# First hidden step by eight plain block products, token parts reordered at block ends, hidden sums widened and all put on VectorE

## The chip, the cores and the metric

The kernel runs on one core of one Trainium2 chip. The metric is the device time of one execution in microseconds (us); lower is better. Three runs of the kernel before gave 1954.87 to 1956.18 us, with a median of 1955.7 us. Engine names are those of the profile: PE is TensorE (PEld its weight load), DVE is VectorE, ACT is ScalarE, POOL is GpSimd, SP is SyncE, which issues the transfers.

## The reference

Each token vector goes through three feed-forward nets (two shared ones and one that its batch entry selects), the three results are weighted by a softmax gate and added to the token, and a linear layer of a chosen category is added on top.

```python
# x: (2, 2048, 512) read as 8 x 512 wide nets of hidden size F = 2048
s0 = relu(x @ swi[0]) @ swo[0]
s1 = relu(x @ swi[1]) @ swo[1]
eo = relu(x @ wi[type_label]) @ wo[type_label]
gate_in = concatenate([eo[:, 0], s0[:, 0], s1[:, 0]])
w = softmax(relu(gate_in @ g1) @ g2)
x = x + (eo * w[0] + s0 * w[1] + s1 * w[2])
out = x + (x @ W[cat_ids] + b[cat_ids])
```

All arrays are float32, and the kernel keeps float32 accuracy by splitting each factor of a product into a high part (rounded to the matmul's fp32r type) and a low part, the rest.

## The kernel before, in words

**Tiling.** The 4,096 tokens are worked in 4 blocks of 1,024. Each block runs through 12 steps: 3 nets by 4 slices of the hidden size, 48 steps `m` in all. A step multiplies tokens by a slice of the first weight matrix (the up products, PSUM banks `ups`), applies relu, and multiplies the hidden values by a slice of the second matrix (the down products, banks `rps`), which is summed into `ACC`.

**Products of blocks.** Every matrix product is done as a 2 by 2 product of blocks with seven block products instead of eight (Winograd's form). That needs sums of blocks on both sides: `XT` and `XS` of tokens, `PUS` and `PDS` of weights, and `HT` of hidden blocks. An up slice is done in two half steps `n = 2m` and `n = 2m + 1` of 512 tokens by 7 products of 6 matmuls each, and a down slice by 7 products of 12 matmuls. A step holds 168 matmuls of 128x512.

**Hidden blocks and their sums.** The seven up products of a half step are put together into four hidden blocks: `hid[:,0]` by a relu on ACT, `hid[:,2]` by `block_22` (L1227) on DVE and a relu, `HT[:,1]` by `block_21` (L1236) and a relu, `hid[:,1]` by a relu. From them `hidden_sum` (L737) makes four sums, `which` = 0 to 3, each of a half step's 128x512: those of half 0 on POOL, those of half 1 on DVE. Sum 1 reads sum 0, and sum 3 reads sum 1. `hidden_high` (ACT, L938) then rounds each of the seven inputs of the down products, 128x1024 for both halves, and `hidden_low` (DVE, L1186) takes the rest.

**Order within a step.** All engines run orders that are written out by hand. In step `m` PE goes through seven slots of two up products (of the half steps `a = 2m + 2` and `b = 2m + 3`, which belong to the next step) and one down product, by turns: `up(a,0)`, `up(a,1)`, `down(m-1,6)`; `up(a,2)`, `up(a,3)`, `down(m,0)`; `up(a,4)`, `up(a,5)`, `down(m,1)`; `up(a,6)`, `up(b,0)`, `down(m,2)`; and so on to `up(b,5)`, `up(b,6)` and `down(m,5)`. `up(a,6)` writes a bank that `block_22(a)` has to have read. `S(m)` below is the time at which `up(a,0)` starts.

On DVE a step is, in order: sums 0, 1 and 3, the preparation of weights where there is one (`up_low` L1166, `up_sums` L1322, `down_low` L1173), `hidden_low` 1, `second(0)` (the adding of `down(m-1,6)` into `ACC`, `add_sum`, L1205 and L1208), sum 2, `hidden_low` 2 and 6, `block_22(a)`, `hidden_low` 3, and so on. `first_product`, `seventh_product` and `chain` are ACT's copies of banks (L884, L890, L896), and L953 is its copy of the first down product of a step.

**Prepared weights.** In the first block, and again in steps 32 to 34 for a part of the weights, the high and low parts and block sums of weights are made on the chip and kept in HBM; later steps load them. POOL makes the sums of the down weights (`down_sums`, L779 to L788).

**Start.** Half step 0 needs no sums: it is done by the eight plain block products (`plain`, weights in `WD`), while the token and weight sums that half step 1 needs by seven products are made. The sums of its weights are made afterwards on POOL from `PF` (`first_up_sums`, L767), for the steps that load them later.

**Block ends.** In the last step of a block (`m` = 11, 23, 35; `start` in the code) the up products are already those of the next block, so its token parts (`token_high` L843, `token_low` L1157, tiles `XH`, `XL`) are made between the other work: `token_low` 3 ahead of the sums, 4 and 5 behind `second(0)`, 6 ahead of `block_22(a)`.

Of the kernel before, what the change touches and what calls it, by code (L numbers as in the profile page):

```python
# [12 lines left out]
P = 128  # L13
# [47 lines left out]

T_COUNT = [(1, 2, 3, 4), (1, 2, 4, 3)]
# [98 lines left out]
X_ORDER_FIRST = [0, 6, 3, 1, 2, 4, 5]  # L161
# [10 lines left out]
B12_USED = 3  # L172
# [27 lines left out]
def build(nc, xT, expert_id, category_id, wi, wo, swi, swo, g1, g2, W, bias, out):  # L200
# [13 lines left out]
    with ctx:  # L214
# [27 lines left out]
        PF = sb("PF", [P, 4, HB], F32, at=hh_at + 5 * 4 * KB)  # L242
# [25 lines left out]
        WS = sb("WS", [P, 4, 2, HB], F32R, at=r_at + 28 * KB)  # L268
        SR = sb("SR", [P, 4, HB], F32, at=r_at + 36 * KB)
# [39 lines left out]
        s_pf = sem("first_blocks_loaded")  # L309
# [26 lines left out]
        s_T = [sem("hidden_sums_0"), sem("hidden_sums_1")]  # L336
# [50 lines left out]
        def _(sp):  # L387
# [50 lines left out]
            def load_up(n, i):  # L438
# [3 lines left out]
                if weight_set(n // 2) == 0 and n % 2 == 0:  # L442
                    sp.wait_ge(s_wsk, 32)
# [114 lines left out]
            sp.dma_start(PF[:, :, :], swi[0, 0, :, :, :]).then_inc(s_pf, 16)  # L558
# [5 lines left out]
            blocks_up(1, None)  # L564
            blocks_up(2, None)
            blocks_down(0, None)
            sp.dma_start(g2s[:, :, :], g2_v).then_inc(s_g2, 16)
            keep_first(0)
            keep_first(1)
# [4 lines left out]
            keep_up(1, 0)  # L574
            keep_up(1, 1)
            blocks_up(3, experts)
# [3 lines left out]
            for m in range(STEPS):  # L580
# [4 lines left out]
                for i in range(PRODUCTS):  # L585
# [5 lines left out]
                    if m == 0 and i == 4:  # L591
                        keep_first_sums()
# [28 lines left out]
                    if True:  # L621
# [28 lines left out]
                        if m == 1 and i == 1:  # L650
                            load_ahead(1)
                        if m in (3, 4, 5) and i == 2:
                            keep_ahead(1, m - 3)
                        if m == 5 and i == 2:
# [65 lines left out]
        def hidden_sum(eng, N, half, which):  # L720

            before = PRODUCTS * (N - 1)
            h11, h12, h22 = (hid[:, q, half, :] for q in range(3))
            if N > 0:
                eng.wait_ge(s_dn, before + (3, 2, 4, 5)[which] + 1)
            if which == 0:
                eng.wait_ge(s_relu, 4 * (2 * N + half) + 4)
                dst, p, q, op = HT[:, 3, half, :], h22, h12, ALU.subtract
            elif which == 1:
                eng.wait_ge(s_T[half], 4 * N + T_COUNT[half][0])  # L730
                dst, p, q, op = HT[:, 2, half, :], HT[:, 3, half, :], h11, ALU.add
            elif which == 2:
                dst, p, q, op = HT[:, 4, half, :], h12, h11, ALU.subtract
            else:
                eng.wait_ge(s_T[half], 4 * N + T_COUNT[half][1])
                dst, p, q, op = HT[:, 5, half, :], HT[:, 1, half, :], HT[:, 2, half, :], ALU.subtract
            eng.tensor_tensor(dst, p, q, op).then_inc(s_T[half], 1)  # L737
# [15 lines left out]

        tail_banks = [aps[:, :], ups[2], ups[0], ups[1], rps[1][:, 0, :], rps[1][:, 1, :], rps[0][:, 0, :], rps[0][:, 1, :]]
# [6 lines left out]
        def _(pool):  # L761
            def first_up_sums():
# [979 lines left out]
```

## Time and profile before

| | |
|---|---|
| median of 3 runs | 1955.7 us (1954.87 to 1956.18) |
| the profiled execution | 1956.29 us |
| its span in the trace | 1954.4 us |
| PE busy | 1933.9 us, 99% |
| DVE busy | 1343.6 us, 69% |
| ACT busy | 981.7 us, 50% |
| POOL busy | 402.1 us, 21% |

The span is the time from the first to the last instruction that the trace shows, and the execution's own time is 1.9 us longer. Busy shares are means over the whole span: DVE is above 85% in the first quarter and near 60% after it. PEclk is the granted clock of PE as a share of its full speed.

### The profile page before, as it was taken

How to read it: one execution, taken by the hardware profiler on the slowest of the kernel's cores; microseconds unless marked ns; L12 is line 12 of the kernel's file. 1: busy time of each engine (PE TensorE's matmuls, PEld its weight loads, DVE VectorE, ACT ScalarE, POOL GpSimd, SP SyncE). 2: the span in 40 equal slices, each digit the busy share in tenths (PEclk: the TensorE clock that was granted, in tenths of full speed). 3: DMA queues.
4: the chain of work that ended last, by engine and by line, in shares of the span. 5: the costliest groups of instructions: out<-in, count | busy, mean ns of one | idle time of the engine just before them, and what ended most of it. 6: DMA issues, size and time to landing. Idle time of an engine off the chain costs nothing.

```text
span 1954.4 us, 25279 instructions
## 1 busy us (share of the span) xinstructions
PE 1933.9 (99%) x8510; PEld 1597.6 (82%) x8510; DVE 1343.6 (69%) x1508; ACT 981.7 (50%) x1438; POOL 402.1 (21%) x283
## 2 busy tenths in 40 slices
PE   7999999999999999999999999999999999999999
PEld 6888888887888888888888888888878888888887
DVE  8888888898576556565655545589975656555566
ACT  5766766756454334444554344456555433344342
POOL 3234224322211111331111111122321111111120
PEclk9999999999999999999999999999999999999999
DMA  6876777768876666786776676578777776656642
GB/s 219 300 292 249 292 279 295 278 242 304 277 256 217 204 204 215 266 293 211 261 258 204 193 224 209 189 278 295 267 279 257 239 228 221 216 182 211 224 156 97
DMA packets 192321, 468.29 MB, mean 240 GB/s; under 512 B 17476, under 2 KB 58436, under 8 KB 185924
## 3 DMA queue, kind: packets, MB, share of 16 engines
q1 hardware_dynamic: 192196, 466.69, 69.8%
q8 instruction: 70, 1.15, 0.2%
q14 instruction: 55, 0.45, 0.1%
HBM read 319.82 MB, written 146.80 MB: 239 GB/s over the span
## 4 chain that ended last, share of the span: by engine, by line
PE 73%; DVE 2%; DMA 1%; issue 1%; ACT 1%; SPq 0%; ACTq 0%; DVEq 0%
PE ups L1555 35%; PE rps L1555 35%; PE aps L1555 3%; DMA XT<-xT_kept 1%; DVE WD L1173 0%; DVE XL L1157 0%; DVE HL L1186 0%; DVE HT L737 0%; ACT XH L843 0%; ACT HH L938 0%; DVE ACC L1205 0%; DVE XT L1512 0%; ACT WD L874 0%; DVE XL L1518 0%; PE aps L1654 0%
## 5 line engine op out<-in xcount | busy, mean ns | idle before, releaser
L1555 PE MATMUL ups<-XH,WU 128*128 128x512 f32 x2660 | 878.0, 391 | 14.1 <-issue 4.4
L1555 PE MATMUL rps<-HH,WD 128*128 128x512 f32 x2672 | 876.5, 389 | 0.6 <-ACT rps L953 0.6
L1555 PEld LDWEIGHTS ups<-XH,WU 128*128 128x128 f32 x2660 | 501.7, 189 | 123.0 <-issue 11.0
L1555 PEld LDWEIGHTS rps<-HH,WD 128*128 128x128 f32 x2672 | 501.3, 188 | 105.4 <-DVE HL L1186 1.3
L1555 PE MATMUL rps<-HL,WD 128*128 128x512 f32 x1336 | 519.7, 389 | 0.0
L1555 PE MATMUL ups<-XL,WU 128*128 128x512 f32 x1330 | 519.3, 390 | 0.0
L737 POOL TENSOR_TENSOR HT<-hid 128x512 f32<-128x512 f32 x96 | 133.2, 1388 | 1316.8 <-PE rps L1555 1298.2
L1186 DVE TENSOR_TENSOR HL<-HT,HH 128x1024 fp32r<-128x1024 f32 x240 | 290.2, 1219 | 9.6 <-ACT HH L938 5.1
L1208 DVE SCALAR_TENSOR_TENSOR ACC<-rps,gw,ACC 128x1024 f32<-128x1024 f32 x126 | 161.6, 1282 | 196.6 <-PE rps L1555 196.3
L1555 PEld LDWEIGHTS rps<-HL,WD 128*128 128x128 f32 x1336 | 251.0, 188 | 52.1
L1555 PEld LDWEIGHTS ups<-XL,WU 128*128 128x128 f32 x1330 | 250.6, 188 | 51.5
L938 ACT ACTIVATE HH<-HT 128x1024 fp32r<-128x1024 f32 x240 | 252.4, 1053 | 26.8 <-DVE HT L737 25.2
L1205 DVE TENSOR_TENSOR ACC<-rps,ACC 128x1024 f32<-128x1024 f32 x124 | 151.4, 1221 | 103.0 <-PE rps L1555 102.9
L912 ACT ACTIVATE HT<-HT 128x512 f32<-128x512 f32 x95 | 60.1, 633 | 276.3 <-DVE HT L1236 276.3
L1227 DVE TENSOR_TENSOR hid<-ups,w 128x512 f32<-128x512 f32 x95 | 65.4, 688 | 123.4 <-PE ups L1555 123.4
L1186 DVE TENSOR_TENSOR HL<-hid,HH 128x1024 fp32r<-128x1024 f32 x96 | 131.3, 1368 | 20.0 <-ACT HH L938 20.0
L904 ACT ACTIVATE hid<-ups 128x512 f32<-128x512 f32 x95 | 56.4, 594 | 117.5 <-PE ups L1555 117.5
L896 ACT ACTIVATE u<-ups 128x512 f32<-128x512 f32 x95 | 56.8, 598 | 105.3 <-PE ups L1555 105.3
L890 ACT ACTIVATE w<-ups 128x512 f32<-128x512 f32 x95 | 55.9, 588 | 102.3 <-PE ups L1555 102.3
L938 ACT ACTIVATE HH<-hid 128x1024 fp32r<-128x1024 f32 x96 | 101.6, 1058 | 1.5
L884 ACT ACTIVATE ups<-ups 128x512 f32<-128x512 f32 x95 | 55.3, 583 | 81.5 <-PE ups L1555 78.3
L908 ACT ACTIVATE hid<-hid 128x512 f32<-128x512 f32 x95 | 60.1, 632 | 68.1 <-DVE hid L1227 68.0
(129 smaller groups left out, 1521.7 us busy)
## 6 DMA issues: line engine op xcount, KB each, us to landing
WU<-wu_kept SPq DMA_DIRECT2D x448, 256.0 KB, 3.5
WD<-wd_kept SPq DMA_DIRECT2D x224, 512.0 KB, 3.3
wd_kept<-WD SPq DMA_DIRECT2D x112, 512.0 KB, 3.5
wu_kept<-WU SPq DMA_DIRECT2D x31, 1024.0 KB, 4.9
wu_kept<-WU SPq DMA_DIRECT2D x31, 768.0 KB, 4.5
sums_kept<-ACC SPq DMA_DIRECT2D x28, 512.0 KB, 5.4
MB<-sums_kept SPq DMA_DIRECT2D x28, 512.0 KB, 5.7
XS<-in_x_dram SPq DMA_DIRECT2D x21, 512.0 KB, 5.8
```

Of the source, the lines that this page charges most:

```text
L737: eng.tensor_tensor(dst, p, q, op).then_inc(s_T[half], 1)
L890: act.activation(w[:, :], ups[2][:, :], ACT.Copy).then_inc(s_w, 1)
L896: act.activation(u[:, :], ups[1][:, :], ACT.Copy).then_inc(s_u, 1)
L904: act.activation(hid[:, 0, half, :], ups[0][:, :], ACT.Relu).then_inc(s_relu, 1)
L908: act.activation(hid[:, 2, n % 2, :], hid[:, 2, n % 2, :], ACT.Relu).then_inc(s_relu, 1)
L912: act.activation(HT[:, 1, n % 2, :], HT[:, 1, n % 2, :], ACT.Relu).then_inc(s_relu, 1)
L938: act.activation(HH[:, i, :, :], src, ACT.Copy).then_inc(s_hhi, 1)
L1186: dve.tensor_tensor(HL[:, i, :, :], src, HH[:, i, :, :].bitcast(F32), ALU.subtract).then_inc(s_hlo, 1)
L1205: dve.tensor_tensor(ACC[:, j, :, :], src[:, :, :], ACC[:, j, :, :], ALU.add).then_inc(s_acc, 1)
L1208: dve.scalar_tensor_tensor(out=ACC[:, j, :, :], in0=src[:, :, :], scalar=gw[:, g:g + 1], in1=ACC[:, j, :, :], op0=ALU.mult, op1=ALU.add).t ...
L1227: dve.tensor_tensor(hid[:, 2, half, :], ups[1][:, :], w[:, :], ALU.add).then_inc(s_ev, 1)
L1555: ins = pe.matmul(dst, stationary[a], moving[c], start=start and j == 0, stop=stop and j == 2, skip_group_check=True)
```

## The change

The diff does three things.

**The first step.** Half step 1 too is done by the eight plain products, from raw blocks of tokens and weights. Its banks are the three `ups` banks and `aps`. That takes 8 products of 6 matmuls where there were 7. `PF` holds the raw blocks of both halves. The block sums of these weights, which later steps load, are now made in steps 0 and 1 for both halves, from blocks that are loaded once more into `SR`: four small sums on POOL, the high parts on ACT, the low parts on DVE. Weights are prepared from half step 2 on. Some loads that look ahead for the second block of tokens come one step later.

**The hidden sums.** `hidden_sum` takes both halves in one instruction of 128x1024, and all of them are on DVE: 4 instructions in a step where DVE had 4 of 128x512 and POOL had 4 of 128x512. POOL keeps `down_sums`, `ahead_sum` and `first_up_sums`. There is one semaphore for the sums where there were two, and `relu_11` and `relu_12` of either half step of the next step now wait for the third of the counts in `T_COUNT`, which is 4, so for all four sums.

**The block ends.** On DVE `second(0)` and `token_low` 4 go ahead of the hidden sums, and `token_low` 5 behind them and ahead of `hidden_low` 1. On ACT `token_high` 5, the copy `w` and the copy `u` move up.

```diff
-X_ORDER_FIRST = [0, 6, 3, 1, 2, 4, 5]
+X_ORDER_FIRST = [0, 6, 3, 1, 2, 5, 4]
...
-        PF = sb("PF", [P, 4, HB], F32, at=hh_at + 5 * 4 * KB)
+        PF = sb("PF", [P, 2, 4, HB], F32, at=hh_at + 4 * 4 * KB)
...
+            def first_blocks_again(n):
+                sp.wait_ge(s_xlo, PRODUCTS)
+                if n > 0:
+                    sp.wait_ge(s_wsl, 2 * n)
+                sp.dma_start(SR[:, :, :], swi[0, n, :, :, :]).then_inc(s_sr, 16)
...
+                    if m < 2 and i == 0:
+                        first_blocks_again(m)
+                    if m < 2 and i == 4:
+                        keep_first_sums(m)
...
-                        if m == 1 and i == 1:
+                        if m == 2 and i == 1:
                             load_ahead(1)
...
-        def hidden_sum(eng, N, half, which):
+        def hidden_sum(eng, N, which):
...
-            h11, h12, h22 = (hid[:, q, half, :] for q in range(3))
+            h11, h12, h22 = (hid[:, q, :, :] for q in range(3))
...
             if which == 0:
-                eng.wait_ge(s_relu, 4 * (2 * N + half) + 4)
-                dst, p, q, op = HT[:, 3, half, :], h22, h12, ALU.subtract
+                eng.wait_ge(s_relu, 8 * (N + 1))
+                dst, p, q, op = HT[:, 3, :, :], h22, h12, ALU.subtract
```

On POOL:

```diff
-            hidden_sum(pool, 0, 0, 0)
-            hidden_sum(pool, 0, 0, 1)
             down_sums(0, False)
-            hidden_sum(pool, 0, 0, 2)
             down_sums(0, True)
             for m in range(STEPS):
                 N, d = m + 1, m
-                hidden_sum(pool, d, 0, 3)
-                if m == 0:
-                    first_up_sums()
+                if m < 2:
+                    first_up_sums(m)
...
-                if N < STEPS:
-                    hidden_sum(pool, N, 0, 0)
-                    hidden_sum(pool, N, 0, 1)
                 if prepared(N):
                     down_sums(N, False)
```

On ACT, in `relu_11` and in `relu_12`:

```diff
-                    act.wait_ge(s_T[half], 4 * (N - 1) + T_COUNT[half][2])
+                    act.wait_ge(s_T, 4 * (N - 1) + T_COUNT[2])
```

On ACT, in a step:

```diff
                 if start:
                     token_high(s + 1, 4)
-                if d >= 0:
-                    hidden_high(d, 3)
-                if more:
+                    token_high(s + 1, 5)
                     seventh_product(a)
+                hidden_high(d, 3)
+                if more and not start:
+                    seventh_product(a)
+                if start:
+                    chain(a)
                 made(m - 1, PRODUCTS - 1)
```

On DVE, in a step:

```diff
                 if start:
                     token_low(s + 1, 3)
-                if d >= 0:
-                    hidden_sum(dve, d, 1, 0)
-                    hidden_sum(dve, d, 1, 1)
-                    hidden_sum(dve, d, 1, 3)
+                    second(0)
+                    token_low(s + 1, 4)
+                hidden_sum(dve, d, 0)
+                hidden_sum(dve, d, 1)
+                hidden_sum(dve, d, 3)
+                if start:
+                    token_low(s + 1, 5)
                 if m > 0 and prepared_half(a):
                     up_low(a, 1)
-                if prepared_half(b):
+                if m > 0 and prepared_half(b):
                     up_sums(b)
                 made(m - 1, PRODUCTS - 1)
                 hidden_low(d, 1)
-                second(0)
-                if start:
-                    token_low(s + 1, 4)
-                    token_low(s + 1, 5)
+                if not start:
+                    second(0)
                 if d >= 0:
-                    hidden_sum(dve, d, 1, 2)
+                    hidden_sum(dve, d, 2)
                     hidden_low(d, 2)
...
-                if m == 0:
-                    first_sums_low(0)
-                    first_sums_low(1)
-                if m in (2, 3, 4):
-                    ahead_sum(dve, 1, m - 2)
+                if m < 2:
+                    first_sums_low(m, 0)
+                    first_sums_low(m, 1)
+                if m in (3, 4, 5):
+                    ahead_sum(dve, 1, m - 3)
```

On PE, at the start:

```diff
-            for p in range(len(PLAIN)):
-                plain(p)
-            for i in range(PRODUCTS):
-                up(1, i)
+            for n in range(2):
+                for p in range(len(PLAIN)):
+                    plain(n, p)
```

How the instructions stand on DVE at the start of step 2, an ordinary step that also prepares weights (`ACC` is the adding of a down product, `HT` the hidden sums, `WU` the low parts and `PUS` the block sums of up weights), is in the next two pieces. Before:

```order
L1205 TENSOR_TENSOR ACC<-rps,ACC 128x1024
L737 TENSOR_TENSOR HT<-hid 128x512
L737 TENSOR_TENSOR HT<-HT,hid 128x512
L737 TENSOR_TENSOR HT<-HT 128x512
L1166 TENSOR_TENSOR WU<-PUR,WU 128x2x256
L1166 TENSOR_TENSOR WU<-PUS,WU 128x2x256
```

And now:

```order
L1210 TENSOR_TENSOR ACC<-rps,ACC 128x1024
L751 TENSOR_TENSOR HT<-hid 128x1024
L751 TENSOR_TENSOR HT<-HT,hid 128x1024
L751 TENSOR_TENSOR HT<-HT 128x1024
L1172 TENSOR_TENSOR WU<-PUR,WU 128x2x256
L1172 TENSOR_TENSOR WU<-PUS,WU 128x2x256
```

The order is the same, and the three sums are twice as wide.

On DVE in the last step of the second block, `m = 23`, from the add ahead of `token_low` 3 to `block_22(a)` (`XL` is `token_low`, `HL` is `hidden_low`), the rows before are:

```order
L1208 SCALAR_TENSOR_TENSOR ACC<-rps,gw,ACC 128x1024
L1157 TENSOR_TENSOR XL<-XT,XH 128x1024
L737 TENSOR_TENSOR HT<-hid 128x512
L737 TENSOR_TENSOR HT<-HT,hid 128x512
L737 TENSOR_TENSOR HT<-HT 128x512
L1186 TENSOR_TENSOR HL<-HT,HH 128x1024
L1208 SCALAR_TENSOR_TENSOR ACC<-rps,gw,ACC 128x1024
L1157 TENSOR_TENSOR XL<-XT,XH 128x1024 x2
L737 TENSOR_TENSOR HT<-hid 128x512
L1186 TENSOR_TENSOR HL<-HT,HH 128x1024
L1186 TENSOR_TENSOR HL<-hid,HH 128x1024
L1157 TENSOR_TENSOR XL<-XS,XH 128x1024
```

The rows in the same place now are:

```order
L1163 TENSOR_TENSOR XL<-XT,XH 128x1024
L1213 SCALAR_TENSOR_TENSOR ACC<-rps,gw,ACC 128x1024
L1163 TENSOR_TENSOR XL<-XT,XH 128x1024
L751 TENSOR_TENSOR HT<-hid 128x1024
L751 TENSOR_TENSOR HT<-HT,hid 128x1024
L751 TENSOR_TENSOR HT<-HT 128x1024
L1163 TENSOR_TENSOR XL<-XT,XH 128x1024
L1191 TENSOR_TENSOR HL<-HT,HH 128x1024
L751 TENSOR_TENSOR HT<-hid 128x1024
L1191 TENSOR_TENSOR HL<-HT,HH 128x1024
L1191 TENSOR_TENSOR HL<-hid,HH 128x1024
L1163 TENSOR_TENSOR XL<-XS,XH 128x1024
```

The second `ACC` row, which needs `down(m-1,6)`, stood behind the sums and `hidden_low` 1 and now stands ahead of them, with one `XL` row behind it; the last row of both pieces is `token_low` 6, and `block_22(a)` comes next.

On POOL the order from its first sums on, before:

```order
L737 TENSOR_TENSOR HT<-hid 128x512
L737 TENSOR_TENSOR HT<-HT,hid 128x512
L786 TENSOR_TENSOR PDS<-PDR 128x512
L788 TENSOR_TENSOR PDS<-PDS,PDR 128x512
L737 TENSOR_TENSOR HT<-hid 128x512
L779 TENSOR_TENSOR PDS<-PDR 128x512
L781 TENSOR_TENSOR PDS<-PDR,PDS 128x512
L737 TENSOR_TENSOR HT<-HT 128x512
```

And now, where `SR` are the sums of the first weights:

```order
L804 TENSOR_TENSOR PDS<-PDR 128x512
L806 TENSOR_TENSOR PDS<-PDS,PDR 128x512
L797 TENSOR_TENSOR PDS<-PDR 128x512
L799 TENSOR_TENSOR PDS<-PDR,PDS 128x512
L785 TENSOR_TENSOR SR<-SR 128x256
L786 TENSOR_TENSOR SR<-SR 128x256
L788 TENSOR_TENSOR SR<-SR 128x256
L790 TENSOR_TENSOR SR<-SR 128x256
```

The `HT` rows are gone from POOL, and nothing stands ahead of the `PDS` rows any more.

## Rows read from the trace of the kernel before

**Rows 1.** The page: busy us, share of the span, instructions.

```profile
PE 1933.9 (99%) x8510; PEld 1597.6 (82%) x8510; DVE 1343.6 (69%) x1508; ACT 981.7 (50%) x1438; POOL 402.1 (21%) x283
```

**Rows 2.** Busy time by stretch; us, each engine, PEclk, DMA share, GB/s.

```profile
23.00:38.00 15.00, 7.42 (x21) 4.91 (x22) 14.97 (x13) 5.24 (x8) 14.84 (x11) 0.85 0.31 105
60.00:457.00 397.00, 397.00 (x1753) 328.78 (x1752) 350.11 (x457) 257.24 (x406) 131.44 (x87) 1.00 0.75 282
...
470.00:474.00 4.00, 3.46 (x8) 2.79 (x9) 4.00 (x6) 4.00 (x7) 0.00 (x0) 0.57 0.26 97
```

**Rows 3.** Timeline of PE at the start; in brackets idle before and releaser.

```profile
18.60 0.39 PE L1555 MATMUL ups<-XH,WU 128*128 128x512 f32 x1
...
25.06 0.47 PE L1555 MATMUL ups<-XH,WU 128*128 128x512 f32 x1 [2.21 <-DVE WU L1166]
...
28.91 0.47 PE L1555 MATMUL ups<-XH,WU 128*128 128x512 f32 x1 [2.22 <-DVE XL L1157]
...
36.79 0.63 PE L1555 MATMUL ups<-XH,WU 128*128 128x512 f32 x1 [2.90 <-DVE hid L1227]
...
43.76 0.50 PE L1555 MATMUL ups<-XH,WU 128*128 128x512 f32 x1 [0.98 <-ACT ups L884]
...
54.77 0.39 PE L1555 MATMUL ups<-XH,WU 128*128 128x512 f32 x1
```

**Rows 4.** Groups by form: count, busy us, mean ns.

```profile
L737 DVE TENSOR_TENSOR HT<-hid 128x512 f32<-128x512 f32 x96 | 69.1, 720 | 0.0
L737 DVE TENSOR_TENSOR HT<-HT,hid 128x512 f32<-128x512 f32 x48 | 37.5, 781 | 4.9
L1186 DVE TENSOR_TENSOR HL<-HT,HH 128x1024 fp32r<-128x1024 f32 x240 | 290.2, 1219 | 9.6 <-ACT HH L938 5.1 <-DVE HT L737 0.5
L737 POOL TENSOR_TENSOR HT<-hid 128x512 f32<-128x512 f32 x96 | 133.2, 1388 | 1316.8 <-PE rps L1555 1298.2 <-ACT HT L1004 18.7
```

**Rows 5.** Timelines of DVE and POOL at the start, where both work.

```profile
24.32 1.73 POOL L786 TENSOR_TENSOR PDS<-PDR 128x512 f32<-128x512 f32 x1
...
24.83 1.77 DVE L1166 TENSOR_TENSOR WU<-PUS,WU 128x512 fp32r<-128x512 f32 x1
```

**Rows 6.** Timelines of step 2: `block_22(a)` on DVE, `up(a,6)` on PE.

```profile
128.37 0.68 DVE L1227 TENSOR_TENSOR hid<-ups,w 128x512 f32<-128x512 f32 x1
...
130.93 0.39 PE L1555 MATMUL ups<-XH,WU 128*128 128x512 f32 x1
```

**Rows 7.** Timelines of steps 5, 9 and 34: the same two places in each.

```profile
241.99 0.68 DVE L1227 TENSOR_TENSOR hid<-ups,w 128x512 f32<-128x512 f32 x1
...
245.17 0.39 PE L1555 MATMUL ups<-XH,WU 128*128 128x512 f32 x1
...
414.11 0.68 DVE L1227 TENSOR_TENSOR hid<-ups,w 128x512 f32<-128x512 f32 x1
...
414.94 0.62 PE L1555 MATMUL ups<-XH,WU 128*128 128x512 f32 x2
...
1397.99 0.69 DVE L1227 TENSOR_TENSOR hid<-ups,w 128x512 f32<-128x512 f32 x1
...
1400.02 0.39 PE L1555 MATMUL ups<-XH,WU 128*128 128x512 f32 x1
```

**Rows 8.** Timelines of step 23: `token_low` 3, `S(23)` and `up(a,6)`.

```profile
943.38 1.23 DVE L1157 TENSOR_TENSOR XL<-XT,XH 128x1024 fp32r<-128x1024 f32 x1
...
941.98 0.39 PE L1555 MATMUL ups<-XH,WU 128*128 128x512 f32 x1
...
958.29 0.39 PE L1555 MATMUL ups<-XH,WU 128*128 128x512 f32 x1
```

**Rows 9.** Timeline of PE in steps 11 and 35: `S`, waits, `up(a,6)`.

```profile
457.35 0.39 PE L1555 MATMUL ups<-XH,WU 128*128 128x512 f32 x1
...
470.55 0.77 PE L1555 MATMUL ups<-XH,WU 128*128 128x512 f32 x1 [2.15 <-issue]
...
477.67 0.39 PE L1555 MATMUL ups<-XH,WU 128*128 128x512 f32 x1
...
1421.78 0.39 PE L1555 MATMUL ups<-XH,WU 128*128 128x512 f32 x1
...
1440.99 0.50 PE L1555 MATMUL ups<-XH,WU 128*128 128x512 f32 x1 [0.57 <-DVE hid L1227]
```

**Rows 10.** Timelines of the last step: `hidden_low` 1 and 3, and PE's wait.

```profile
1910.62 2.36 DVE L1186 TENSOR_TENSOR HL<-HT,HH 128x1024 fp32r<-128x1024 f32 x2
...
1911.90 0.50 PE L1555 MATMUL rps<-HH,WD 128*128 128x512 f32 x1 [0.62 <-ACT rps L953]
```

More of the change, by code:

```diff
@@ L930, in hidden_high @@
                     if i == 1:
-                        act.wait_ge(s_relu, relus + 3)
+                        act.wait_ge(s_relu, relus + (3 if N > 0 else 4))
                     else:
-                        for half in range(2):
-                            act.wait_ge(s_T[half], 4 * N + T_COUNT[half][{3: 0, 2: 1, 4: 2, 5: 3}[i]])
+                        act.wait_ge(s_T, 4 * N + T_COUNT[{3: 0, 2: 1, 4: 2, 5: 3}[i]])
                     src = HT[:, i, :, :]
-                if N == 0 and i == 5:
-                    act.wait_ge(s_S0, 4)
                 act.activation(HH[:, i, :, :], src, ACT.Copy).then_inc(s_hhi, 1)
@@ L1061, in _ @@
                     token_high(s + 1, 4)
-                if d >= 0:
-                    hidden_high(d, 3)
-                if more:
+                    token_high(s + 1, 5)
                     seventh_product(a)
+                hidden_high(d, 3)
[3 more added lines that the diff above has]
+                    chain(a)
                 made(m - 1, PRODUCTS - 1)
-                if d >= 0:
-                    hidden_high(d, 2)
-                if start:
-                    token_high(s + 1, 5)
+                hidden_high(d, 2)
                 second(0)
-                if more:
+                if more and not start:
                     chain(a)
@@ L1182, in hidden_low @@
                 if i in after:
-                    for half in range(2):
-                        dve.wait_ge(s_T[half], 4 * N + T_COUNT[half][after[i]])
+                    dve.wait_ge(s_T, 4 * N + T_COUNT[after[i]])
                 src = hid[:, 0 if i == 0 else 2, :, :] if i in (0, 6) else HT[:, i, :, :]
@@ L1349, in _ @@
             token_low(0, 3)
+            for k in range(4):
+                first_up_low(1, k)
             token_sum(dve, 0)
             token_sum(dve, 1)
-            up_sums(1)
             token_low(0, 1)
-            up_low(1, 0)
+            up_sums(2)
             token_low(0, 2)
+            up_low(2, 0)
+            up_low(2, 1)
+            token_sum(dve, 3)
+            token_low(0, 5)
             token_sum(dve, 2)
-            token_sum(dve, 3)
-            up_low(1, 1)
+            up_sums(3)
             token_low(0, 4)
-            token_low(0, 5)
-            up_sums(2)
-            block_22(1)
-            block_21(1)
-            up_low(2, 0)
             hidden_low(0, 0)
-            up_low(2, 1)
             down_low(0, 0)
@@ L1584, in up, with plain @@
                 ins.then_inc(s_up, 1)
-            def plain(p):
+            def plain(n, p):
                 _, slot, i, c = PLAIN[p]
```

247 lines of the change are left out of this document (126 added, 121 removed).

## The prediction

> **What bounds the kernel now.** I read the page first. PE is busy 99% of the span and DVE 69% [rows 1]. The table by stretch then says where PE is not busy: from 60 to 457 us it works all 397.00 us, with DVE busy 350.11 us of them [rows 2]. There 1,753 matmuls take 397 us, so 226.5 ns each; a product of 6 takes 1.36 us, one of 12 takes 2.72 us, and a step of 168 takes 38.08 us. All that can be won is PE's idle and slow time: 1,956.3 us less 8,510 matmuls at 226.7 ns (1,929.2 us) is 27 us, start and end of the execution included. All that can be lost is cover: in the first block DVE has 12% to spare, and a step's DVE chain ends a little ahead of the matmul that needs it.
>
> I then followed PE's timeline at the start [rows 3]. `up(1,0)` starts at 18.60 and `up(2,6)` at 54.77. In between PE waits 2.2 us for `WU` (25.06), 2.2 for `XL` (28.91), 2.9 for `block_22` (36.79) and 1.0 for a bank's copy (43.76). From 23 to 38 us PE is busy 7.42 of 15.00 us while DVE is busy 14.97, and the granted clock is 0.85 [rows 2], which is part of it at the lower level of 1.2 GHz. PE had been idle half of that time before it fell.
>
> Last I looked for the slack of `block_22(a)` in each step. It ends (start plus duration) 129.05 in step 2, and `up(a,6)` starts at 130.93: slack 1.88 [rows 6]. In step 5 it is 2.50, in step 9 `up(a,6)` is the second of the two matmuls in the row at 414.94, so 415.17, and the slack is 0.38, and in step 34 it is 1.34 [rows 7]. Read in the same way, step 1 has 2.49, steps 3, 4, 7 and 8 have 1.74 to 1.86, step 6 has 1.88 and step 10 has 0.40.
>
> **The wider sums.** DVE has now 4 sums of 128x1024 where it had 4 of 128x512. The first three took 720, 781 and about 730 ns one behind the other; no sum of 128x1024 is in the trace, but `hidden_low`, also two SBUF inputs and 128x1024, takes 1,219 ns [rows 4]. Three of these and 0.1 for their dependence make 3.8 us for 2.23, so +1.5. The fourth adds 1.22 less 0.72, and with the overlap of ends +0.54. All four stand ahead of `block_22(a)`: **+2.05 us** to its chain in each step. POOL loses 4 of some 1.39 us in a step, which nobody waited for in the ordinary steps.
>
> The Trainium skill ("Perfetto Trace Analysis", Optimizing Scalar/DVE Operations) says that larger operations help where the engine is saturated, and that where it isn't but causes bubbles on others, smaller ones may get work done sooner. Here the trace says that DVE is not saturated after the first block; by the rule alone the change would cost its 2.05 us in the steps of the later blocks too, some 30 times, or 60 us; by the rows those steps have more slack than that.
>
> In an ordinary step without preparation (blocks 2 and 4, and block 3 but for its last steps) the slack of `block_22(a)` stands mostly near 3.2 us with idle time of DVE ahead of it, and the 2.05 us cost nothing. In the first block:
> - Steps 2, 3, 4, 6, 7, 8: 2.05 against 1.74 to 1.88 is 0.2 short, and a stop of PE costs some 0.15 more for its restart. 6 x 0.4 = **+2.4**. Bounds 0 (the sums cost 0.2 less each time) and 4.
> - Step 5: 2.05 is under 2.50, nothing.
> - Step 1: slack 2.49, but POOL now makes the second half's `SR` sums there. A DVE instruction with two SBUF inputs that runs beside POOL took 1.77 us instead of 0.69, and POOL's own 1.73 [rows 5]: some 1.1 each, of which one or two fall ahead of `block_22`. 2.05 + 1.6 - 2.49 + 0.15 = **+1.3**.
> - Step 9: 2.05 - 0.38 = 1.67, **+1.6**. Step 10: its chain starts 1.6 late today, and 2.05 falls mostly in that: **+0.3** (up to 1.7).
> - Steps 32 to 34, where weights are prepared again: 0.2, 0.8 and 0.9 (2.05 less 1.34, and a restart) [rows 7], **+1.9**.
>
> **The start.** The eight plain products of half 1 need only raw parts, of which `XL` and `WD` come early, so PE runs through them: 18.60 + 8 x 1.36 = 29.5 us. One product more than before is +1.36. Then come `up(2,0)` to `up(2,5)`. These wait for the relus (about 33.0) and for the copy of the first product (about 37.5), since ACT and DVE make the weights of half 2 first. DVE's work ahead is what it was, less `up_sums(1)` and `up_low(1)`, and POOL's four `PDS` sums each stretch a DVE instruction by 1.1 as now. Walking DVE's and ACT's new orders with the durations of the old rows, `up(2,6)` comes at 49.7 where it was 54.77 [rows 3]: -5.0 us. The SR sums in step 0 are in that with 1.5. But PE waits twice in it, for 3 to 4 us, and a lower clock will follow as it does now; I take 0.8 for it: **-4.2**. Bounds: -9.5 (PE's 36.17 us from 18.60 to 54.77 hold 25.9 us of work and 1.36 more are added, less 10.3 of waiting; nearly all of it goes), and -1.
>
> **The block ends.** Before, at step 23, `up(a,6)` started 16.31 us after `S` (958.29 less 941.98), with no wait [rows 8]. Now DVE: `token_low` 3 starts at S+1.40 and ends at 2.55; `second(0)` needs `down(22,6)`, which ends at S+5.44 and is seen at 5.64, so DVE is idle for 3.1 us that it used for the sums. Then at pitches of 1.14 (1.20 for the add): add 6.84, `token_low` 4 at 7.98, three sums 11.6, `token_low` 5 at 12.75, `hidden_low` 1 at 13.9, sum 2 at 15.0, `hidden_low` 2 and 6 at 17.3, `token_low` 6 at 18.45, `block_22` at 19.2. `up(a,5)` comes due at S+12.24 and waits 0.6 for `token_low` 5. `relu_11` waits for sum 2, and the ACT copies of the first down product queue behind it, so `down(23,1)` starts at about S+16.4 instead of 13.6. Both ways `up(a,6)` starts near S+19.3: **+3.1**.
>
> At steps 11 and 35 the same chain has two `down_low` of 0.6 more, and ends near S+20.5. Before, `up(a,6)` started at S+20.32 in step 11 (477.67), after a wait of 2.3 us for `token_low` 4 (470.55) and a granted clock of 0.57 from 470 to 474 us [rows 2, 9], and at S+19.21 in step 35 (1440.99). DVE gets about 1 us back there, as POOL's own sums no longer stretch its `down_low`; I keep that for the bound. **+0.3 and +1.3**. Bounds for the three: 0 and 8 (a clock at 1.2 GHz behind each wait, as it costs 1.7 us in step 11 today).
>
> **The tail.** PE waits in the last step for `hidden_low` 1, which starts 1910.62 and lasts 1.22; PE resumes at 1911.90 [rows 10]. Three wider sums ahead of it: **+1.4**.
>
> **Sum.** -4.2 + 2.4 + 1.3 + 1.6 + 0.3 + 1.9 + 3.1 + 0.3 + 1.3 + 1.4 = +9.4 us. On the profiled execution, 1956.3, it gives 1965.7; that execution lies 0.6 above the median of the runs, 1955.7, so I say **1965.0**.
>
> **Rival A: faster, 1947.** The start gives its bound of 9.5, and the slack in the first block holds, because the chain ahead of `block_22` is rid of POOL: where POOL worked at the same time, a DVE instruction took up to 1.1 longer [rows 5], and POOL's own sums of hidden blocks, 1.39 us each [rows 4], now make no such stretch; one in a step pays for half of the widening. The block ends then give back what they lose today: 2.3 and 1.7 in step 11, some 2 in step 35. -9.5 - 4 + 5 for steps 9, 23 and the tail is -8.5. It decides if in step 2 `up(a,6)` follows its predecessor without a wait. Against it: the sums on DVE have means of 720 to 781 ns [rows 4], which are not stretched, so there is little to give back. The Trainium skill ("GPSIMD Engine Reference", 1. Specifications) says that GpSimd shares SBUF interfaces with VectorE and that VectorE instructions with two SBUF inputs contend; the 1.77 us agrees. By it alone each sum taken off POOL helps. Chance 0.18.
>
> **Rival B: no change, 1956.** The sums cost 1.7 instead of 2.05, so that steps 2 to 8 lose nothing (-2.4), the start gives 7 (-2.8), and the block ends lose half (-2.3). +1.9. Chance 0.13.
>
> **Rival C: slower by more, 1972.** The delay of the wait for all four sums by `relu_11` moves on: ACT's queue behind it (copies of down product, `hidden_high`) is late in every step of the first block, and each of PE's stops there at a block end is followed by the lower clock: 3 x 1.7 and 0.3 more in each of 8 steps. +9.4 + 7. Chance 0.12. My forecast, from +4 to +13, has 0.57.
>
> **How the numbers follow.** This kernel's runs differ by 0.07%; what can't be told from no change is 0.2% or 3.9 us (1951.8 to 1959.6). Faster has A, 0.18; same has B, 0.13; slower has the forecast and C, 0.69. The range leaves out the better half of A and the worst of C: 1949 to 1971.
>
> **What would show it.** Right if the timeline of the new kernel shows `up(2,6)` near 49.7 us; `up(a,6)` waiting for `block_22` by 0.2 to 0.3 in steps 2 to 4 and 6 to 8, and by 1.6 in step 9; idle time of DVE of about 3 us ahead of the add in step 23 and `up(a,6)` 19.3 us after `S`; PE's wait in the last step 1.4 longer; busy DVE near 1,343.6 + 48 x 2 = 1,440 us. It goes wrong first at the start, where my walk rests on orders of two engines that have never run so, then by the widened sums, whose 0.2 shortfall in six steps is the difference of two numbers ten times as large, and at the block ends if `second(0)` is not late.

## The result and the profile after

The changed kernel takes 1973.24 us (median of 4 runs, 1971.78 to 1974.08), beside 1955.94 us for the kernel before (now the median of 4 runs). The ratio is 1.0091, with a 95% interval of 1.0078 to 1.0104: slower by 17.3 us. The forecast of 1965.0 us had the sign, and its range ended at 1971.

The profiled execution took 1974.08 us and its span is 1972.3 us. First the page, with the columns of [rows 1]:

```profile
PE 1945.5 (99%) x8516; PEld 1597.9 (81%) x8516; DVE 1412.0 (72%) x1504; ACT 979.2 (50%) x1437; POOL 134.1 (7%) x95
```

DVE has 68 us more work and POOL 268 us less; PE has the 6 matmuls more of the eighth product. The forecast of 1,440 us for DVE was 28 too high: it left out what DVE gets back when POOL doesn't slow it. Added up over all forms of DVE's instructions, the time above the usual duration of the form is 71 us before and 45 us after, 26 less.

Busy time by stretch, as in [rows 2]:

```profile
23.00:38.00 15.00, 11.45 (x50) 8.86 (x49) 13.25 (x18) 8.82 (x14) 0.26 (x1) 1.00 0.18 72
57.00:62.00 5.00, 4.22 (x12) 3.06 (x13) 4.85 (x9) 4.16 (x8) 0.00 (x0) 0.69 0.85 256
478.00:490.00 12.00, 8.60 (x36) 6.18 (x35) 12.00 (x13) 7.91 (x12) 0.00 (x0) 1.00 0.60 206
951.00:971.00 20.00, 17.53 (x76) 13.65 (x76) 16.29 (x15) 11.43 (x16) 0.00 (x0) 1.00 0.60 196
1926.00:1933.00 7.00, 4.94 (x15) 3.57 (x15) 4.62 (x4) 3.80 (x5) 0.00 (x0) 0.76 0.29 99
```

The start went as the forecast said: from 23 to 38 us PE is busy 11.45 us instead of 7.42, and the group with `up(2,6)` starts at 50.23 us (49.7 forecast, 54.77 before). But there is a stretch at a low clock behind 57 us (0.69) and one in the tail (0.76) that the kernel before doesn't have.

PE's timeline at the places of [rows 3, 6, 9, 10], where the last bracket names the wait:

```profile
44.80 0.39 PE L1560 MATMUL ups<-XH,WU 128*128 128x512 f32 x1
...
57.78 0.50 PE L1560 MATMUL ups<-XH,WU 128*128 128x512 f32 x1 [1.95 <-DVE HT L1241]
...
99.89 0.80 PE L1560 MATMUL ups<-XH,WU 128*128 128x512 f32 x1 [2.03 <-DVE HT L1241]
...
134.48 0.50 PE L1560 MATMUL ups<-XH,WU 128*128 128x512 f32 x1
...
411.77 0.50 PE L1560 MATMUL ups<-XH,WU 128*128 128x512 f32 x1 [0.15 <-ACT ups L893]
...
423.21 0.50 PE L1560 MATMUL ups<-XH,WU 128*128 128x512 f32 x1 [0.26 <-DVE hid L1232]
...
483.27 0.47 PE L1560 MATMUL rps<-HH,WD 128*128 128x512 f32 x1 [2.46 <-ACT rps L959]
...
967.85 0.47 PE L1560 MATMUL rps<-HH,WD 128*128 128x512 f32 x1 [1.85 <-ACT rps L959]
970.70 0.40 PE L1560 MATMUL ups<-XH,WU 128*128 128x512 f32 x1
...
1928.51 0.50 PE L1560 MATMUL rps<-HH,WD 128*128 128x512 f32 x1 [2.06 <-DVE HL L1191]
```

The row at 44.80 is the group of up products that started at 49.33 before: 4.5 us ahead. The group at 57.78 stood at 60.21 before and the one at 99.89 at 98.29: the lead is gone within two steps, at waits for `block_21`, L1241, of which the forecast had none.

Setting each start of a group of up products beside the same one of the kernel before gives the account. The differences of the changed kernel's lag between these places are:

| place | forecast, us | measured, us |
|---|---|---|
| start, to the end of the down product behind `up(2,5)` | -4.2 (or -5.0 without clock) | -4.5 |
| steps 0 and 1 | +1.3 | +7.9 |
| steps 2 to 10 | +4.3 | +5.5 |
| step 11 | +0.3 | +0.5 |
| step 23 | +3.1 | +3.1 |
| steps 32 to 34 | +1.9 | +1.5 |
| step 35 | +1.3 | +1.2 |
| tail | +1.4 | +3.0 |
| sum | +9.4 | +18.2 |

Behind the last of these groups 0.3 us come back: the spans differ by 17.9 us.

Here is the chain behind 57.78 us. POOL's, ACT's and DVE's timelines, in that order:

```profile
47.60 0.74 POOL L785 TENSOR_TENSOR SR<-SR 128x256 f32<-128x256 f32 x1 [24.34 <-DMA SR<-in_L_cond_swi_dram]
48.30 1.72 POOL L786 TENSOR_TENSOR SR<-SR 128x256 f32<-128x256 f32 x1
49.98 1.18 POOL L788 TENSOR_TENSOR SR<-SR 128x256 f32<-128x256 f32 x1
51.24 1.60 POOL L790 TENSOR_TENSOR SR<-SR 128x256 f32<-128x256 f32 x1
...
52.88 1.16 ACT L1005 ACTIVATE WS<-SR 128x512 fp32r<-128x512 f32 x2 [4.21 <-POOL SR L790]
53.94 1.04 ACT L944 ACTIVATE HH<-HT 128x1024 fp32r<-128x1024 f32 x1
54.88 1.00 ACT L970 ACTIVATE ACC<-rps 128x1024 f32<-128x1024 f32 x1
55.79 0.62 ACT L883 ACTIVATE WD<-PDR 128x512 fp32r<-128x512 f32 x1
...
56.44 0.69 DVE L1179 TENSOR_TENSOR WD<-PDR,WD 128x512 fp32r<-128x512 f32 x1 [4.19 <-ACT WD L883]
57.04 0.69 DVE L1241 TENSOR_TENSOR HT<-ups,u 128x512 f32<-128x512 f32 x1
```

The re-loaded blocks land at 47.6 us. POOL's four sums end at 52.84. The load was issued at 39.38. ACT, which works in program order, stands 4.21 us for them with `down_high` (L883) queued behind; DVE stands 4.19 us for that with `block_21(2)` (L1241) queued behind; PE stands 1.95 us for `block_21(2)`, and the clock falls. In step 1 the same four engines do the same from 90.6 to 99.89 us.

### The profile page after: what moved, and what is told of

Read it like the earlier page. It is cut to its first block, busy times and chain, and to the rows that moved or that the text cites. A ratio compares the mean times of both kernels' runs of the same rounds, so it can differ in the third digit from the quotient of the medians.

```text
span 1972.3 us, 24767 instructions
## 1 busy us (share of the span) xinstructions
PE 1945.5 (99%) x8516; PEld 1597.9 (81%) x8516; DVE 1412.0 (72%) x1504; ACT 979.2 (50%) x1437; POOL 134.1 (7%) x95
## 4 chain that ended last, share of the span: by engine, by line
PE 84%; DVE 11%; issue 2%; DMA 1%; ACT 1%; POOL 1%; SPq 0%; DVEq 0%; ACTq 0%
PE ups L1560 40%; PE rps L1560 40%; PE aps L1560 3%; DVE HT L751 3%; DVE HL L1191 2%; DVE WU L1172 1%; DVE WD L1179 1%; DMA SR<-in_L_cond_swi_dram 1%; DVE ACC L1210 1%; DVE hid L1232 0%; DMA HT<-in_x_dram 0%; DVE XL L1163 0%; DVE PUS L1328 0%; DVE PUS L1331 0%; DVE PUS L1329 0%
## 5 line engine op out<-in xcount | busy, mean ns | idle before, releaser
L1560 PEld LDWEIGHTS ups<-XH,WU 128*128 128x128 f32 x2632 | 496.2, 189 | 128.8 <-ACT ups L893 8.0
L1191 DVE TENSOR_TENSOR HL<-hid,HH 128x1024 fp32r<-128x1024 f32 x96 | 125.5, 1308 | 9.2 <-ACT HH L944 9.2
L751 DVE TENSOR_TENSOR HT<-hid 128x1024 f32<-128x1024 f32 x96 | 116.9, 1217 | 0.0
```

Source lines behind the costliest of these rows:

```text
L751: eng.tensor_tensor(dst, p, q, op).then_inc(s_T, 1)
L1191: dve.tensor_tensor(HL[:, i, :, :], src, HH[:, i, :, :].bitcast(F32), ALU.subtract).then_inc(s_hlo, 1)
L1560: ins = pe.matmul(dst, stationary[a], moving[c], start=start and j == 0, stop=stop and j == 2, skip_group_check=True)
```

## The experiments

Each kernel was timed beside the kernel before on the same chip; the medians of before were 1955.6 to 1955.8 us. A difference to the changed kernel's 1973.24 us is one between two such timings. Numbers by step come from the one profiled execution of each kernel.

**First weights' sums later.** In steps 0 and 1 ACT's and DVE's parts of these sums move behind `relu_12(a)`:

```diff
-                if m < 2:
-                    first_sums_high(m, 0)
-                    first_sums_high(m, 1)
                 if d >= 0:
                     hidden_high(d, 5)
...
                     if prepared_half(b):
                         up_high(b, 1)
+                if m < 2:
+                    first_sums_high(m, 0)
+                    first_sums_high(m, 1)
```

> The changed kernel (1973.2 us) with one thing moved: the high and low parts of the first weights' block sums (ACT first_sums_high, DVE first_sums_low) stand behind relu_12(a) and ahead of second(3) in steps 0 and 1 instead of ahead of hidden_high 5, and their keeping one slot later. My theory: in steps 0 and 1 ACT stands 4.2 us for the SR sums of POOL, which wait for a re-load, and DVE's down_low and block_21(a) stand behind ACT; PE lost 3.95 us in step 0 and 3.9 in step 1 by it (wait and lower clock). Then some 7.5 us go: 1965.7 us, and PE's waits of 2.1 and 2.2 us near 57 and 99 us are gone. Rival: block_21 is late there because of the wider hidden sums and POOL's slowing of DVE; then the time stays within 1.5 us of 1973.

Measured: 1966.14 us (1964.88 to 1967.81), ratio 1.0053 [1.0039, 1.0067], 7.1 us less than the changed kernel, where 7.5 were expected. The rival is out: steps 0 and 1 lose 0.6 us instead of 7.9. ACT's and DVE's timelines show what became of the wait (in these rows `HT` L1241 is `block_21(2)`):

```profile
51.95 0.62 ACT L883 ACTIVATE WD<-PDR 128x512 fp32r<-128x512 f32 x1
...
52.61 0.84 DVE L1179 TENSOR_TENSOR WD<-PDR,WD 128x512 fp32r<-128x512 f32 x1 [0.31 <-ACT WD L883]
53.38 0.68 DVE L1241 TENSOR_TENSOR HT<-ups,u 128x512 f32<-128x512 f32 x1
```

`block_21(2)` runs at 53.38 instead of 57.04, and PE's two waits are gone. POOL's sums end at the same time as before the edit.

**Hidden sums of half 0 back on POOL**, start and block ends as changed (the `hidden_sum` of the kernel before, its calls and its two semaphores).

```diff
             for m in range(STEPS):
                 N, d = m + 1, m
+                hidden_sum(pool, d, 0, 3)
                 if m < 2:
                     first_up_sums(m)
...
+                if N < STEPS:
+                    hidden_sum(pool, N, 0, 0)
+                    hidden_sum(pool, N, 0, 1)
```

> The changed kernel with the hidden sums as before: those of half 0 on POOL, those of half 1 on DVE, each 128x512, with the two semaphores. Start and block ends stay changed. My theory: the wider sums cost 0.6 us in each of steps 2 to 10, 1.5 in steps 32 to 34, 1.5 to 3 in the tail and some at the block ends: 9 to 11 us less, so 1962 to 1964 us, with block_21 still late in steps 0 and 1. Rival: the sums on POOL now queue behind the first weights' sums, which wait for a re-load, and slow DVE; then steps 0 and 1 lose 3 us more and the whole comes to 1967 or above.

Measured: 1962.02 us (1960.8 to 1963.91), ratio 1.0034 [1.0021, 1.0048]: 11.2 us less, just above the 9 to 11 of the theory. Nothing is lost in steps 5 to 10, 32 to 34 and the tail, and step 23 loses 1.0 instead of 3.1. The rival is out: steps 0 and 1 lose 4.5 us, less than the changed kernel and not 3 more. But the start gains nothing either: PE stands 1.0 us behind the kernel before where the changed kernel was 4.5 ahead. That speaks of a second effect of the move, which the next but one shows.

**Block ends of before**, wide sums kept. ACT's order goes back too; the cut shows DVE's.

```diff
                     token_low(s + 1, 3)
-                    second(0)
-                    token_low(s + 1, 4)
                 hidden_sum(dve, d, 0)
                 hidden_sum(dve, d, 1)
                 hidden_sum(dve, d, 3)
-                if start:
-                    token_low(s + 1, 5)
...
-                if not start:
-                    second(0)
+                second(0)
+                if start:
+                    token_low(s + 1, 4)
+                    token_low(s + 1, 5)
```

> The changed kernel with the order of DVE and ACT at the block ends as before, wide sums kept on DVE. My theory: the new order costs 3.1 us in step 23 alone, and helps in steps 11 and 35, where the wide sums ahead of token_low 4 would otherwise add 1.5 us to PE's wait: -2.9, +1.5 and +0.8, so 1972.6 us. Rival: the new order is what costs at all three block ends (4.9 us in all), and the time falls to 1968.3.

Measured: 1966.77 us (1964.83 to 1969.7), ratio 1.0059 [1.0045, 1.0073]. My number (1972.6) is out; the rival's (1968.3) had the cause right and was 1.5 us too high. The new order costs 6.5 us by the medians and 5.5 by the steps. I had the wide sums delay `token_low` 4 in steps 11 and 35. They do, but DVE comes to that chain earlier, as POOL no longer slows it (two `down_low` ahead of it in step 11 take 1.28 us instead of 2.89), and PE's wait for `token_low` 4 there is 1.3 us instead of 2.2: steps 11, 23 and 35 lose -0.8, +0.2 and -0.1 us beside the kernel before, where the changed kernel loses 0.5, 3.1 and 1.2.

**The new start alone**, both other parts as before.

> The kernel before with the new start alone: half step 1 by eight plain products, the first weights' sums in steps 0 and 1; hidden sums and block ends as before. My theory: 4.5 us are won up to up(2,6) and 7.9 lost behind it in steps 0 and 1 to ACT's wait for the sums: 1955.9 + 3.4 = 1959.3 us. Rival: the loss in steps 0 and 1 comes from the wider sums; then it is 1951.5 us.

Measured: 1961.74 us (1961.24 to 1963.02), ratio 1.0035 [1.0021, 1.0049]; the rival (1951.5) is out, and the theory's 1959.3 was 2.4 us too low. Up to 49.33 us of the old timeline it wins 2.5 us, not 4.5, and loses 4.8 in step 0, with ACT standing 5.04 us for POOL's `SR` sums. Step 1 loses 1.6 and steps 2 to 4 another 1.5, which the kernel before does not; its cause stays open. The DVE timeline of this kernel at the start, POOL's beside it, and DVE's in the changed kernel for the same three instructions:

```profile
27.16 2.31 DVE L714 TENSOR_TENSOR XT<-HT 128x1024 f32<-128x1024 f32 x1
30.60 2.33 DVE L1171 TENSOR_TENSOR XL<-XT,XH 128x1024 fp32r<-128x1024 f32 x1 [1.12 <-ACT XH L861]
32.85 2.28 DVE L714 TENSOR_TENSOR XT<-XS 128x1024 f32<-128x1024 f32 x1
```

```profile
26.65 1.73 POOL L751 TENSOR_TENSOR HT<-hid 128x512 f32<-128x512 f32 x1
28.35 2.25 POOL L797 TENSOR_TENSOR PDS<-PDR 128x512 f32<-128x512 f32 x1
30.57 1.27 POOL L799 TENSOR_TENSOR PDS<-PDR,PDS 128x512 f32<-128x512 f32 x1
31.81 2.24 POOL L751 TENSOR_TENSOR HT<-HT 128x512 f32<-128x512 f32 x1
```

```profile
26.74 1.21 DVE L714 TENSOR_TENSOR XT<-HT 128x1024 f32<-128x1024 f32 x1
29.08 1.22 DVE L1163 TENSOR_TENSOR XL<-XT,XH 128x1024 fp32r<-128x1024 f32 x1 [1.13 <-ACT XH L852]
30.22 1.22 DVE L714 TENSOR_TENSOR XT<-XS 128x1024 f32<-128x1024 f32 x1
```

With POOL at work beside it each takes 1.1 us longer. Each of the three ends 1.1 us after the end of a POOL instruction that had begun before it (28.38, 31.84 and 34.05 us), about its own undisturbed time: it looks as if it stood until POOL was done, and was not merely slowed. Two of the four POOL rows are hidden sums; the other two are `PDS` sums, which in the changed kernel have nothing ahead of them and are done from 17.41 to 23.26 us, before this place. So the move of the hidden sums to DVE helps the new start. By how much differs between executions: with the sums on DVE seven kernels with this start are 3.5 to 6.1 us ahead at this place (four of them, with the same orders up to there, 3.9 to 6.1), with those of half 0 on POOL one is 2.5 ahead and the other 1.0 behind. The Trainium skill ("GPSIMD Engine Reference", 1. Specifications) says that the two engines share SBUF interfaces and that VectorE instructions with two SBUF inputs contend; these rows agree, 1.21 against 2.31 us.

**The wide sums alone**, in the kernel before.

> The kernel before with one thing changed: the hidden sums as in the changed kernel, 128x1024 and all on DVE. Theory: the wider sums cost in the old kernel what they cost in the changed one outside the start: 5.5 us in steps 2 to 10, 1.5 in steps 32 to 34, 3.0 in the tail, -0.7 at the block ends: +9.3, less some 2 us that DVE wins at the start where POOL no longer slows it: 1963 us. Rival (the sums cost nothing where DVE has idle time; the later first block's loss came from the new start's backlog): 1956 us.

Measured: 1960.56 us (1959.81 to 1964.01), ratio 1.0028 [1.0017, 1.0039]. The rival is out; the theory's 1963 was 2.4 us too high. The parts: -3.8 us at the start up to 54.77 (2 were expected) and +0.6 in steps 0 and 1; +5.4 in steps 2 to 10; -1.2 in step 11; +0.2 in step 23; +1.4 in steps 32 to 34; +0.7 in step 35; +1.4 in the tail. The tail's +1.4 is the forecast's own number; the clock, which fell behind the longer wait of the changed kernel (0.76 from 1926 to 1933), accounts for the rest of its 3.0: PE's wait here is the same 2.06 us, and the granted clock stays at 1.00.

**The early add behind the sums**, in the changed kernel.

```diff
                     token_low(s + 1, 3)
-                    second(0)
                     token_low(s + 1, 4)
                 hidden_sum(dve, d, 0)
                 hidden_sum(dve, d, 1)
                 hidden_sum(dve, d, 3)
                 if start:
+                    second(0)
                     token_low(s + 1, 5)
```

> The changed kernel with one thing moved at the block ends: the early add (second(0)) goes behind hidden sums 0, 1 and 3, token_low 4 stays ahead of them. DVE then does not stand 3.0 us in step 23 and 1.3 in step 11 for down(m-1,6). Theory: the idle time ahead of the early add is the whole cost of the new block ends: -3.1 us in step 23, -1.3 to -3.3 in steps 11 and 35 each: about 1967 us, as with the old order (1966.8). Rival: what costs is relu_11's wait for all four sums, with the copies of the first down product behind it (PE's wait of 2.0 to 2.6 us for them); then it stays above 1971.

Measured: 1971.06 us (1970.27 to 1974.66), ratio 1.0077 [1.0064, 1.0091]. Neither expectation holds as it was put: the time is just above the rival's 1971, but one of the three block ends went as the theory said. In step 23 the loss falls from 3.1 to 0.6 us, as the theory said. Here is what the changed kernel had there, on DVE:

```profile
956.92 1.28 DVE L1213 SCALAR_TENSOR_TENSOR ACC<-rps,gw,ACC 128x1024 f32<-128x1024 f32 x1 [3.02 <-PE rps L1560]
```

and here PE's wait in the experiment, which was 1.85 us:

```profile
968.36 0.47 PE L1560 MATMUL rps<-HH,WD 128*128 128x512 f32 x1 [0.31 <-ACT rps L959]
```

In steps 11 and 35 nothing is won. In step 11 the idle time was only 1.3 us and DVE's chain gets 0.7 us shorter, since `token_low` 4 now waits for its high part, and PE still stands 2.45 us for the copies on ACT, behind `relu_11`, behind sum 2; then in this execution the clock fell. In steps 0 and 1, which the edit doesn't touch, this profiled execution lost 12.6 us where that of the changed kernel lost 7.9, after a start that won 6.1 instead of 4.5, so its whole time says little on the ends. The medians differ by 2.2 us, which step 23 alone explains. The steps say: idle time before the early add is the cost in step 23; in steps 11 and 35 it is the length of the chain up to sum 2 and `relu_11`.

**A kernel from the parts that win.** New start, late sums of the first weights, block ends of before; the hidden sums of half 0 on DVE in steps 0 and 1 (128x512) and on POOL from step 2. The cut is shown against the kernel with all of half 0 on POOL.

```diff
-                hidden_sum(pool, d, 0, 3)
+                if d > 1:
+                    hidden_sum(pool, d, 0, 3)
...
+                if d < 2:
+                    hidden_sum(dve, d, 0, 0)
                 hidden_sum(dve, d, 1, 0)
```

> The new start (eight plain products twice) with the first weights' sums late in steps 0 and 1, block ends as before, the half 0 hidden sums of steps 0 and 1 on DVE (128x512) and from step 2 on on POOL as before. Theory: the start gains only while POOL stays away from DVE there (in the changed kernel 4.5 us up to the end of half 1's plain products and the first seven-part ones, 2.5 where POOL makes the sums), and nothing of the first block's loss is left: 1955.6 - 3.4 = 1952.2 us. Rival: steps 1 to 4 lose 0.3 to 0.6 us each as they do in the two kernels with sums on POOL, by whatever cause: 1954 us.

Measured: 1952.76 us (1951.54 to 1955.1, 11 runs), ratio 0.9986 [0.9977, 0.9995]: faster than both kernels, nearer the theory's 1952.2 than the rival's 1954. What the rival said of the steps is there: steps 1 to 4 lose 0.3, 0.6, 0.6 and 0.2 us, at `block_22`, with a cause that stays open. A second measurement:

> The hybrid kernel once more, beside the one above on the same chip: 1952.8 us, as in its first run (1951.5 to 1955.1).

gave 1953.3 us, ratio 0.9987 [0.9978, 0.9996].

**All sums on DVE, narrow and early.** As above, but POOL has none of the hidden sums; those of half 0 numbered 0 to 2 stand ahead of the last add of the step before.

```diff
+                hidden_sum(dve, N, 0, 0)
+                hidden_sum(dve, N, 0, 1)
+                hidden_sum(dve, N, 0, 2)
                 second(6)
```

> As the hybrid kernel, but all hidden sums on DVE in pieces of 128x512, and sums 0, 1 and 2 of half 0 ahead of the last add of the step before, where DVE stands 1.1 to 2.2 us for PE. Theory: ahead of block_22(a) stand then only 0.6 us more than before, under the slack of 1.7 to 1.9, and POOL no longer slows DVE: no loss in steps 2 to 8, 0.4 in step 9, and the block ends win 0.7: 1952 us. Rival: that idle time is needed; the add comes late, and with it the chain: 1957 us or more.

Measured: 1955.73 us (1953.93 to 1956.48), ratio 0.9998 [0.9989, 1.0007]. It is neither the theory's 1952 nor the rival's 1957. The first half of the theory held: no step up to 8 loses anything, and PE is 5.2 us ahead at the start of step 9. DVE's timeline at the end of step 1 shows the three early sums where DVE stood for PE before:

```profile
108.46 0.68 DVE L751 TENSOR_TENSOR HT<-hid 128x512 f32<-128x512 f32 x1
109.23 0.69 DVE L751 TENSOR_TENSOR HT<-HT,hid 128x512 f32<-128x512 f32 x1
109.85 0.68 DVE L751 TENSOR_TENSOR HT<-hid 128x512 f32<-128x512 f32 x1
110.45 1.22 DVE L1210 TENSOR_TENSOR ACC<-rps,ACC 128x1024 f32<-128x1024 f32 x1
```

The second half fell: steps 9 to 11 lose 1.6 us, steps 32 to 34 1.6, step 35 0.8 and the tail 0.3. The Trainium skill ("Perfetto Trace Analysis", Optimizing Scalar/DVE Operations) says that where an engine isn't saturated but causes bubbles on others, breaking up instructions may let work finish sooner; steps 2 to 8 agree (3.5 us lost with 128x1024, none with pieces of 128x512, of which three are early), though width and place were changed together here.

**The same up to step 8, POOL from step 9 on.**

> As the all-VectorE kernel with early narrow sums (1955.7 us), but from step 9 on the half 0 sums are on POOL as before. In that kernel nothing was lost up to step 9 (5.0 us ahead of the kernel before at 419 us), and 4 us afterwards, in steps 9 to 11, 32 to 35 and the tail; in the hybrid (sums on POOL from step 2) 1.8 us were lost in steps 1 to 4 and nothing from there. Theory: both causes are of their stretch, and the parts add up: 1955.7 - 5.3 = 1950.4 us. Rival: POOL's sums slow DVE when they set in at step 9, where the slack is least (0.38 us), and 1 to 2 us are lost there: 1952 us.

Measured: 1951.69 us (1950.33 to 1953.27, 11 runs), ratio 0.9978 [0.9969, 0.9987], the fastest of all: 4.1 us under the kernel before and 21.5 under the changed one. The median is between the two numbers expected, nearer the rival's 1952, and the profiled execution shows the rival's loss: nothing up to step 9, then 1.2 us in step 9, where POOL's sums set in and PE waits for `block_22(b)`. In these rows, DVE's and then PE's, the first instruction takes 0.75 us without POOL:

```profile
405.32 1.78 DVE L1273 SCALAR_TENSOR_TENSOR gacc<-G,yv,gacc 128x512 f32<-128x512 f32 x1
...
412.68 0.50 PE L1575 MATMUL ups<-XH,WU 128*128 128x512 f32 x1 [0.87 <-DVE hid L1239]
```

That execution, at 1953.27, is the slowest of the eleven; its start won 3.5 us where that of the kernel above won 5.2.

## Why the forecast was wrong

**Step that failed: "The SR sums in step 0 are in that with 1.5", and with it "+1.3" for step 1.** I priced POOL's sums of the first weights by how much they slow a DVE instruction beside them. What they cost is a wait: they start when a re-load has landed (47.6 us), and ACT, which takes their result in its program order, holds up `down_high`, DVE's `down_low`, `block_21` and PE. Steps 0 and 1 lost 7.9 us where I had 1.3. The shift of the sums' users alone gave back 7.1, and steps 0 and 1 then lose 0.6. It is shown by that experiment and by the chain of rows. I followed `block_22` in each step and stopped the walk of step 0 at `up(2,6)`; the chain that was late was one slot further on. Of the 8.8 us by which the sum was short, 6.6 are this, and about half of the 7.9 is the lower clock behind each of the two waits (1.8 and 1.7 us of slow matmuls).

**The start, -4.2:** right in size (-4.5 here; 3.9, 4.0 and 6.1 won in three other kernels with the same orders up to there), so the last 0.3 is luck. The raw products run through as forecast, but I had written that POOL's `PDS` sums stretch DVE there "as now": they are done by 23.26 us, and that is part of the gain. With the hidden sums on POOL 2.5 us was the most that was won. The bound of -9.5 rests on a wrong sum: 102 matmuls from 18.60 to 54.77 are 23.1 us of work, not 25.9, and idle and slow time are 13.1, not 10.3.

**Wider sums, +2.05 for each chain against the slack:** right, but for step 9. Step 5 loses nothing, steps 2 to 4 and 6 to 8 lose 0.45 to 0.6 where 0.4 was forecast, step 10 0.6 (0.3), steps 32 to 34 1.5 (1.9). Step 9 loses 1.4 where 1.6 was forecast, and that is luck: the matmul at 415.17, which I read as `up(a,6)` with a slack of 0.38, is `up(b,6)` in the seventh group. `up(a,6)` stood at 397.49 with a slack of 2.49, and in the changed kernel it starts at 404.33 without a wait. The 1.4 are 0.2 at `block_21(a)`, 0.6 up to the next group, most of it at ACT's copy (411.77), and 0.6 at `block_22(b)` (423.21). In the other steps the loss is in three pieces of 0.15 to 0.3 at three successive groups of up products, not one; the kernel before with wide sums alone loses 5.4 in steps 2 to 10.

**Block ends, +3.1, +0.3 and +1.3:** right in size (3.1, 0.5 and 1.2). Both ways that I named, the late `token_low` 5 (PE waits 0.6 us at 964) and `relu_11` with the copies behind it (1.85), show in step 23, where `up(a,6)` starts 19.4 us after `S` as worked out. What I believed of the alternative was wrong: the old order with wide sums costs nothing: it even wins 0.7 us in sum, so 5.5 us by the steps are the price of the new order with wide sums. With narrow sums the new order costs nothing (1962.0 against 1961.7 us). The start alone costs 6.1 us and the wide sums alone 4.8; together they cost 11.1, nearly their sum in the whole, though not step by step.

**The tail, +1.4:** too small in size. The wait grew by 1.4 as forecast, but the clock fell behind it, which it had not done before: 0.76 for 7 us. It comes to 3.0.

**The rivals:** A fails at its own test, since `up(a,6)` in step 2 waits. C has the right sign for the surplus, but its mechanism, `relu_11`'s wait carried through each step of the first block, doesn't show; ACT's queue was held up by another wait, twice. Its number, 1972, is nearest to what was measured, and my range, said to leave out only the worst of C, ended below it. In rival A the sums of steps 9, 23 and the tail are 6.1, not 5, and what the block ends give back adds up to 6, not 4; both together move it by 1 us.

## What to carry over

Of a small side job that waits for a transfer, cost not only what it takes but what is queued behind its user on each in-order engine, and walk on until the lead has reached an engine's next wait. Moved work has two prices, on the engine that gets it and on the engine that the old owner slowed down: here the move of the hidden sums to VectorE cost 4.8 us net with the old start and ends and 11.2 with the new, although the new start won more with it, and only a split by stretch (VectorE where POOL disturbs it, POOL where VectorE's slack is short) beat both kernels. An early add is no gain if the engine has to stand for its input.

## What the runs showed of the hardware

A wait of PE of 2.0 us was followed by matmuls at the low clock in some places (57.8 and 99.9 us, tail: PEclk 0.66 to 0.76) and not in others: behind the 2.46 us at 483.27 the granted clock stayed at 1.00 in the changed kernel, and with the early add moved or the first weights' sums late it fell behind a wait of 2.45 or 2.46 us at the same place. The tail's wait of 2.06 us was followed by it in the changed kernel and not in the kernel before with wide sums. What decides it stays open. It makes the same stall cost 2 or 4 us.

A VectorE instruction with two SBUF inputs took 1.1 us longer beside GpSimd at 128x512 (0.69 to 1.77, 0.75 to 1.78) and at 128x1024 (1.21 to 2.31) alike. One that reads a PSUM bank did not: in the last kernel the add of `rps` into `ACC` that starts at 410.15 us, with GpSimd at work from 409.76 to 411.39, took 1.21 us.
